# Second layer's nodes: ScalarE takes both roots one step later; third layer's nodes: TensorE's output map one step later

## The reference

```python
# second layer (index 1): per relation r and head h, then bias, residual, two normalisations
alpha = e_exp / (e_sum[dst] + 1e-08)
out_rel = segment_sum(alpha * h[src]);  out = out + out_rel           # 4 relations
out = out + bias + x
out = (out - mu) * rsqrt(var + LN_EPS) * ln_gamma + ln_beta
x = _layernorm(x + out)
# third layer (index 2): attention over the edges and the node itself, then its output map
attn_out = agg.reshape(n, D) @ out_w.T + out_b
x = _batchnorm(src + attn_out, g1, b1)       # mean and variance over all nodes
ff = leaky_relu(x @ lin1_w.T + lin1_b) @ lin2_w.T + lin2_b
x = _batchnorm(x + ff, g2, b2);  x = _layernorm(src + x)
```

## Time and profile before

| what | us |
|---|---|
| median of 3 runs | 5833.3 (5829.07 to 5839.89) |
| profiled execution, its own time | 5845.01 |
| its span, first to last instruction | 5843.3 |
| `layer1_nodes`, from VectorE's first instruction to the next stage's first | 2912.8 to 3043.3 |
| `layer2_nodes`, GpSimd's first gather to the first normalisation's scale | 4282.0 to 4342.3 |

### The profile page before, as it was taken

One profiled execution on the slowest core, in us unless ns is written; L12 is line 12 of the kernel. 1 busy time (PEld: TensorE's weight loads), 2 busy tenths in 40 slices (PEclk: granted clock), 3 DMA queues, 4 the chain that ended last, 5 costly groups with the idle time before them and its releaser, 6 DMA issues. The chain is left out here.

```text
span 5843.3 us, 58382 instructions
## 1 busy us (share of the span) xinstructions
PE 2193.6 (38%) x11784; PEld 1214.6 (21%) x11977; DVE 3630.4 (62%) x7119; ACT 2710.8 (46%) x5807; POOL 3279.4 (56%) x2937
## 2 busy tenths in 40 slices
PE   4699999986100000000040000000044655555565
PEld 3355544443000000000020000000022333333333
DVE  8465665654677777777745777787755444444444
ACT  0588878872266666666431222222224333333332
POOL 0788888872755566555246666666514444444443
PEclk9899999998555555555565555555577788888887
DMA  9655555553355555555434555555422222222221
GB/s 387 152 104 102 101 104 93 104 122 77 105 201 203 220 206 211 205 212 202 181 126 141 184 184 172 180 192 182 158 69 72 73 73 78 72 73 72 71 71 58
DMA packets 281953, 816.71 MB, mean 140 GB/s; under 512 B 62437, under 2 KB 177653, under 8 KB 269554
## 3 DMA queue, kind: packets, MB, share of 16 engines
q1 hardware_dynamic: 102828, 561.89, 25.7%
q0 software_dynamic: 169776, 248.56, 19.4%
q10 hardware_dynamic: 9238, 5.24, 0.4%
HBM read 366.96 MB, written 448.51 MB: 140 GB/s over the span
## 5 line engine op out<-in xcount | busy, mean ns | idle before, releaser
L642 POOL DMA_INDIRECT tab<-arena x560 | 949.4, 1695 | 206.7 <-issue 138.9
L2435 POOL DMA_INDIRECT arena<-table,arena x622 | 596.4, 959 | 718.6 <-ACT arena L2462 530.5
L1570 PE MATMUL psum<-ident,arena 128*128 128x128 f32 x15 | 3.7, 428 | 2647.9 <-DVEq L1598 2647.9
L1945 POOL DMA_INDIRECT arena<-table,arena x784 | 749.0, 955 | 417.8 <-issue 261.5
L2521 PE MATMUL psum<-arena 128*128 128x256 bf16 (+1 forms) x3969 | 759.0, 344 | 529.8 <-issue 482.4
L772 PE MATMUL psum<-arena 128*128 128x512 bf16 (+1 forms) x4592 | 920.3, 355 | 6.9 <-issue 1.1
L1330 POOL DMA_INDIRECT arena<-table,arena x588 | 614.9, 1046 | 321.5 <-issue 178.7
L2521 PEld LDWEIGHTS psum<-arena 128*128 128x128 bf16 x4050 | 408.4, 101 | 877.1 <-issue 637.1
L1570 PEld LDWEIGHTS psum<-ident,arena 128*128 128x128 f32 x15 | 2.7, 213 | 2648.6 <-DVEq L1598 2648.3
L772 PEld LDWEIGHTS psum<-arena 128*128 128x128 bf16 x4704 | 432.5, 99 | 470.3 <-issue 19.0
L1377 ACT ACTIVATE arena<-arena 128x128 f32<-128x128 f32 x1344 | 424.9, 389 | 176.1 <-issue 131.1
(11 more groups left out here) (426 smaller groups left out, 5605.0 us busy)
## 6 DMA issues: line engine op xcount, KB each, us to landing
rows<-arena SPq DMA_DIRECT2D x56, 3808.0 KB
arena<-seg_rows SPq DMA_DIRECT2D x112, 896.0 KB
rows<-arena SPq DMA_DIRECT2D x56, 1008.0 KB
seg_rows<-arena SPq DMA_DIRECT2D x28, 1792.0 KB
rows<-arena SPq DMA_DIRECT2D x56, 896.0 KB
arena<-table,arena POOLq DMA_INDIRECT x1994
arena<-src_lanes SPq DMA_DIRECT2D x56, 448.0 KB
tab<-arena POOLq DMA_INDIRECT x560
```

The lines of the kernel that those rows point to most:

```text
L642: eng.indirect_dma_start(out=m.tabs[j], out_offset=bass.IndirectOffsetOnAxis(ap=idx[g][:, k:k + 1], axis=0), in_=rows[g][:, k, 0:D], in_of ...
L1945: eng.indirect_dma_start(out=kv[k][:, j, :], out_offset=None, in_=m.table2, in_offset=bass.IndirectOffsetOnAxis(ap=idx[k][:, j:j + 1], axi ...
L2435: eng.indirect_dma_start(out=feat[h][:, j, :], out_offset=None, in_=m.table3, in_offset=bass.IndirectOffsetOnAxis(ap=idx[h][:, j:j + 1], a ...
```

## The change

```diff
@@ layer1_nodes, scalar @@
-                in_turns((exponentials, lambda k: root(0, k), lambda k: root(1, k), norm_behind, turned, keys_values))
+                in_turns((exponentials, None, lambda k: root(0, k), lambda k: root(1, k), norm_behind, turned, keys_values))
@@ layer2_nodes, tensor @@
-                in_turns((values, output_map))
+                in_turns((values, None, output_map))
```

## The result

The changed kernel takes **5812.94 us** (median of 20 runs, 5799.25 to 5825.11), the kernel before 5831.6 (median of 20, 5811.56 to 5845.06). The ratio is 0.9967, 95% interval 0.9958 to 0.9976: by it 19.2 us shorter, between 14.0 and 24.5 (the two medians differ by 18.7). The forecast time was 5819.5, inside a range from 5812; the forecast difference of 13.8 us lies just under the interval.

What follows compares the result with a forecast made beforehand. No engine is always busy: VectorE's ring waits for late exponentials in the second layer's nodes, and TensorE and ScalarE alternate in the third's. Terms -11.7 and -2.1 make -13.8 us, from 5833.3 to 5819.5, range 5812 to 5828.

Steps and rivals of the forecast that it cites:

- The ring: Second layer's nodes: VectorE's cycle falls from 13.63 to 11.65 us as six waits for exponentials go; 11.7 us gained.
- What is queued behind the moved wait: ScalarE, second layer's nodes: evictions, copy and norm_behind now follow the exponentials' wait; costed at nothing.
- the cover: ScalarE, second layer's nodes: 3.3 us before the first root is due; without it, 1.6 us lost in four cycles.
- Gain whole at the barrier: Second layer's nodes: the end follows the last relations by the same chain, so the whole gain reaches the barrier.
- Output map: Third layer's nodes: TensorE's map one chunk behind, long waits as they stand; last sums 2.1 us earlier.
- The sum: Whole kernel: -11.7 for the exponentials and -2.1 for the output map make -13.8 us.
- The gathers set the pace: Rival, third layer's nodes: gathers pace the stage, 2.4 us lost; -9.3 in all, 5824.0 us; chance 0.28.
- The clock stays up: Rival, second layer's nodes: shorter gap keeps TensorE at 2.4 GHz, up to 3.4 us more, 5816; chance 0.14.
- The gain is given back: Rival: ScalarE's later turned and norm_behind meet an uncovered wait, 6.4 us lost; 5826 us; chance 0.09.
- slower by a late release: Rival, either changed stage: new 14.25 us late TensorE result, map loses 2.4; +5.0, 5838.3 us; chance 0.07.

Runs made afterwards that it cites:

- second profile of the changed kernel, the third with the changed kernel: Both edits again, against the kernel before at 5887.64 us: 5869.25 us, ratio 0.9971 (0.9952 to 0.9991).
- The first comparison: Changed kernel, both edits, against the kernel before at 5831.6 us: 5812.94 us, ratio 0.9967 (0.9958 to 0.9976).
- the one at the other level: Both edits again, against the kernel before at 4797.32 us: 4792.08 us, ratio 0.9984 (0.9966 to 1.0002).
- the first edit: Only ScalarE's exponentials one chunk ahead, against the kernel before: 4785.75 us, ratio 0.9979; on another chip 4797.48 us, ratio 0.9969.

## Why the prediction was right, and where it was not

- **The ring, 11.7 us.** Right in mechanism and size. Forecast 11.65 us a cycle, measured 11.62 on average, over cycles of 10.90 to 12.48: the forecast took TensorE's sum as constant, and it alternates about the same mean. (By the earlier trace rows `relations` is 3.55 us up to the start of `exponents` and the stretch from there to the sum 6.08, where the working has 3.65 and 5.98; the total is the same.) From first to last L1812 the ring went from 81.2 to 69.7 us, 11.5 less; against the 82.2, 82.8, 83.5 and 81.5 us that other profiles of the old order show, and 69.6 to 70.0 of the new, it is 11.5 to 14. The wait fell to 0.3 us where some 0.5 was forecast.
- **What is queued behind the moved wait, nothing.** Right in the changed kernel: the root came with no visible delay. That the cover is a real one, and thin, the roots one more step later showed: 13 to 16 us.
- **Gain whole at the barrier.** Right, and a little more: the stage was 13.6 us shorter, 11.5 of it in the ring, 2.8 between the last L1812 and the last L1853 (23.8 to 21.0) and 0.2 ahead of the ring, less 0.8 behind the last L1853. The 2.8 were not in the sum. They are of the size of one wait: VectorE's L1853 at 3026.24 had waited 7.00 us for a map that TensorE had ended at 3022.85, and the longest wait of that line in the changed kernel is 4.7. At the higher level the three profiles of the old order all show 23.8 us in that stretch, with a wait of 7.0, and the two of the changed kernel 21.0 without it; at the level of 4800 us it is 18.8 and 18.8 against 20.4, 20.4 and 18.8. So at the higher level the gain goes with the edit, at the lower it is nothing or a loss; that the edit removes the wait was not tried apart.
- **Output map, 2.1 us.** This is the term that was mis-sized: the stage won 0.7 us, or 0.2 in the second profile of the changed kernel (72.4). The step that failed is "the first map still starts at 4309.8, the second at 4318.04", with 2.03 us for every map: two waits of unknown cause were carried over as if nothing could move them. ScalarE's first sums did come as before (47.4 us into the stage, 47.1 before). But the wait before the first values fell from 10.80 to 5.20 us and the one before the first sums grew from 6.96 to 13.43 us, so that TensorE's first map came early, the engine was idle for 8.72 us just ahead of the second one, and did that at the low clock, 1.8 us longer, with ScalarE waiting for it. First to last L2218 came to 21.6 us, not 20.6. The two other profiles at this level with the new order show the same: 4.70 and 7.97 us idle, then a second map of 3.8 us, and 21.7 and 21.6 us from first to last. That the first sums came as before is partly luck, since the gathers took 32.8 us and not 31.3. The long waits are tied to them: in the kernel before, in the two profiles of the changed one and in that with the roots one more step later, the second wait ends 3.5, 2.3, 2.4 and 1.9 us after the last gather's instruction.
- **The sum, 13.8 us.** The stages give 13.6 + 0.7 = 14.3, but not as forecast: the map gave 1.4 less, a wait that was in no term 2.8 more, and the end of the stage took 0.8 back. That the total is so near is luck in this part. The first comparison measured 19.2 (14.0 to 24.5), the third with the changed kernel 17 (5 to 28), the one at the other level 7.7 (-1 to 16). The stages' 14.3 lies in each of the three; whether the first has 5 us more than that from the change isn't told by any run, and untouched stages differ by 30 us between single profiles.
- **The gathers set the pace (+2.4 in the third layer's nodes).** Wrong. At the level of 4800 us, where the long waits are missing and the gathers run, two profiles with the old order have 63.0 and 63.1 us for the stage and four with the new 61.2 to 61.5: 1.4 to 1.9 shorter, not longer. The premise fell: VectorE waits 0.2 to 1.4 us in all for gathers there, and its products come 3.5 to 5.6 us apart. Much of the 1.4 to 1.9 may be the clock: the old order has its first map at the low clock in both profiles (3.7 and 3.8 us), and in the profile without gathers, where that map takes 2.0 us with the old order too, the new order gains nothing.
- **The clock stays up.** Not in the three profiles of the changed kernel. The gap came out at 2.66 us as forecast (2.6), in the last two full cycles only; the clock fell under the first of these sums and some 0.5 us ahead of the second, and they took 5.4 and 5.1 us. In one profile of the first edit it did stay up: 3.70 us for the sum, a cycle of 10.43 as the rival had it (10.4), and then the slow one of 12.39 that took it back. So the rival counted as gained for good a cycle that the next one gave back. The Trainium skill, page "TensorE: Matmul & The Clock Gate", section "HAM oscillation — how this bites in real kernels", says that waits between bursts of matmuls let the clock fall each time; for gaps of 2.66 us the traces agree in the changed kernel, where the fall came once only after the next sum had begun, and disagree in that one cycle, where it didn't come.
- **The gain is given back; slower by a late release.** Neither. The late release did grow, 6.96 to 13.43 us, past the 9.3 from which that rival was to decide, but in place of the first one and not on top: 10.80 + 6.96 = 17.8 before, 5.20 + 13.43 = 18.6 after, and 8.66 + 9.42 = 18.1 in the second profile of the changed kernel.

## What to carry to other kernels

Where an engine with an order of its own serves two customers in a cycle, look at when each input was ready and when it was taken: one that stood ready ten microseconds behind a wait for something else is moved ahead by one empty position, and the price is read from what is then queued behind it. One step was enough here and two undid it, so the slack on both sides is worth counting before the depth is chosen. A wait whose cause the profile doesn't show should not be carried over into a forecast as fixed; take it away in a trial, or give the term that leans on it a range of its own size.

## What the runs showed of the hardware that was not expected

**The same kernel at two levels.** The kernel before took 5831.6, 5887.64, 4797.32 and 4810.24 us (medians of 16 to 35 runs) in four comparisons, both levels among them on one chip (5887.64 and 4797.32), and within a comparison its runs lie within 0.7%. The difference lies in the stages over edges (fourth layer's: 1355 and 848 us). GpSimd's gathers of that stage, first in the kernel before at the higher level, then in the first edit alone at the lower one (busy us, mean ns, then idle before them and its releasers):

```profile
L2435 POOL DMA_INDIRECT arena<-table,arena x622 | 596.4, 959 | 718.6 <-ACT arena L2462 530.5 <-issue 186.7 <-ACT arena L2449 0.8
```

```profile
L2435 POOL DMA_INDIRECT arena<-table,arena x622 | 626.2, 1007 | 200.8 <-issue 184.6 <-ACT arena L2462 12.6 <-DVE psum L2561 2.7
```

The gathers are about as long in both; at the higher level they wait 530 us for ScalarE, which in turn stands in waits such as this one for a result of TensorE (27 of them, 751 us in all, against 214 us at the lower level):

```profile
4704.85 0.81 ACT L2503 ACTIVATE arena<-psum 128x768 f32<-128x768 f32 x1 [27.87 <-PE psum L2521]
```

This result is not taken late; TensorE has only just ended it (4689.74 + 15.07 = 4704.81). It is TensorE that was held up, in order of time and then by line, in the kernel before and in the first edit alone:

```profile
4677.10 0.37 PE L2521 MATMUL psum<-arena 128*128 128x256 bf16 x1 [2.23 <-issue]
...
4689.74 15.07 PE L2521 MATMUL psum<-arena 128*128 128x512 bf16 x81 [1.73 <-issue]
```

```profile
L2521 PE MATMUL psum<-arena 128*128 128x256 bf16 (+1 forms) x3969 | 759.0, 344 | 529.8 <-issue 482.4 <-DVE arena L2548 41.3 <-DVE arena L2554 1.8
L2521 PE MATMUL psum<-arena 128*128 128x256 bf16 (+1 forms) x3969 | 672.7, 329 | 108.4 <-DVE arena L2554 63.2 <-DVE arena L2548 41.4 <-issue 0.4
```

From 4674 to 4690 its matmuls start one by one, 2.1 to 2.8 us apart, with no wait that the profile names; GpSimd's gathers run until 4685.96, and the 81 matmuls of the last row follow close behind one another. The idle time of this kind is 482 us at the higher level and 0.4 at the lower, where the gathers run just the same.

**Results of TensorE that come late while gathers run.** In the third layer's nodes at that level ScalarE took a finished map 9.8 us late, and the waits ended 1.9 to 3.5 us after the last gather's instruction; without gathers they were gone and the stage was 11.5 us shorter. In the fourth layer's edges it is TensorE's matmuls that come late, not the taking of a result; leaving out the gathers was not tried there, so that they are the cause is not shown. Why the same gathers do this at one level and not at the other stays open: no run brought the level about.
